# Attention scores of a graph layer: one gather of each pair released a pair earlier, and two products of constants between two groups of products

## The reference

```
xl = (x @ Wl).reshape(-1, HEADS, C)
xr = (x @ Wr).reshape(-1, HEADS, C)
h = jax.nn.leaky_relu(xl[src] + xr[dst], NEG_SLOPE)
e = jnp.einsum('ehc,hc->eh', h, att)
m = jax.ops.segment_max(e, dst, num_segments=N_NODES)
...
msg = alpha[..., None] * xl[src]
out = jax.ops.segment_sum(msg, dst, num_segments=N_NODES)
```

## Time and profile before

| | |
|---|---|
| median of 3 runs | 1267.71 us (1265.4 to 1268.62) |
| the profiled execution | 1267.25 us, its span 1265.2 us |
| score stage, first to last DVE weighting (L1497) | 231.79 to 498.06 us |
| granted TensorE clock over the span | 0.882 |

### The profile page before, as it was taken

How to read it: one execution, slowest core, us unless ns; L and a number is a source line. 1 busy time by engine, 2 the same in 40 slices (tenths; PEclk the granted TensorE clock), 3 DMA queues, 4 the chain that set the end, 5 groups by cost and what they waited for, 6 DMA issues and landing times.

```text
span 1265.2 us, 15650 instructions
## 1 busy us (share of the span) xinstructions
PE 1103.2 (87%) x4847; PEld 815.4 (64%) x4847; DVE 1028.0 (81%) x1458; ACT 678.8 (54%) x1257; POOL 455.9 (36%) x412
## 2 busy tenths in 40 slices
PE   4979878667777775399999999699999999999998
PEld 2578456555556564255555555488888889889896
DVE  8999999778777887899999999876767769573934
ACT  4601200566565663388888888766564674232320
POOL 2072062666665666267777775000002100000000
PEclk9989989676665665599999999799999999999999
DMA  5000000666666667166676776400000111000002
GB/s 189 34 10 15 26 10 7 168 174 175 176 179 169 174 175 183 37 189 194 194 195 195 196 195 142 142 1 26 1 9 26 65 54 31 1 28 15 1 1 83
DMA packets 43434, 122.82 MB, mean 97 GB/s; under 512 B 7838, under 2 KB 8626, under 8 KB 43352
## 3 DMA queue, kind: packets, MB, share of 16 engines
q0 software_dynamic: 29184, 93.81, 28.0%
q1 hardware_dynamic: 14168, 27.98, 6.6%
HBM read 116.13 MB, written 5.59 MB: 96 GB/s over the span
## 4 chain that ended last, share of the span: by engine, by line
PE 46%; ACT 19%; DVE 14%; DMA 7%; issue 7%; POOL 4%; ACTq 1%; SPq 1%; DVEq 0%; POOLq 0%
PE bank L851 11%; PE bank L811 8%; PE bank L797 8%; ACT counts L1037 7%; PE bank L867 7%; DMA arena<-left_table,arena 7%; PE bank L654 5%; POOL arena L570 4%; ACT hot L924 4%; ACT arena L922 4%; PE bank L705 3%; ACT bank L1010 2%; DVE counts L1252 2%; PE bank L759 2%; PE bank L770 1%
## 5 line engine op out<-in xcount | busy, mean ns | idle before, releaser
L570 POOL DMA_INDIRECT arena<-left_table,arena x352 | 375.7, 1067 | 206.2 <-issue 101.6
L759 PE MATMUL bank<-arena,hot 128*128 128x512 f32 x352 | 177.6, 620 | 4.0 <-DVE den_parts L1587 4.0
L705 PE MATMUL bank<-xr_hi,hot_t 128*128 x176 | 114.1, 649 | 73.1 <-ACT bank L1010 50.1
L1497 DVE SCALAR_TENSOR_TENSOR arena<-bank,arena 128x1024 f32<-128x1024 f32 x88 | 107.8, 1225 | 52.3 <-PE bank L705 32.6
L1010 ACT ACTIVATE bank<-arena 128x1024 f32<-128x1024 f32 x88 | 90.4, 1028 | 95.3 <-DMA arena<-left_table,arena 87.3
L851 PE MATMUL bank<-counts_r,ns 128*128 128x512 f32 (+2 forms) x720 | 137.1, 349 | 0.0
L851 PEld LDWEIGHTS bank<-counts_r,ns 128*128 128x128 f32 x720 | 125.6, 188 | 10.4
L1037 ACT ACTIVATE counts<-bank 128x1280 f32 x88 | 108.9, 1238 | 35.0 <-issue 25.8
L770 PE MATMUL bank<-arena 128*128 128x512 bf16 x528 | 113.1, 351 | 0.5 <-ACT counts L1037 0.3
L1499 DVE TENSOR_REDUCE arena<-arena 128x16 f32<-128x1024 f32 x88 | 107.4, 1220 | 3.0
L705 PEld LDWEIGHTS bank<-xr_hi,hot_t 128*128 128x128 f32 x176 | 50.2, 285 | 92.2 <-issue 84.5
(11 more groups left out here) (248 smaller groups left out, 2193.8 us busy)
## 6 DMA issues: line engine op xcount, KB each, us to landing
arena<-left_table,arena POOLq DMA_INDIRECT x352
arena<-in_x_dram SPq DMA_DIRECT2D x18, 256.0 KB, 4.6
arena<-in_L_gnn_W_dram SPq DMA_DIRECT2D x8, 512.0 KB
arena<-in_L_gnn_W_dram SPq DMA_DIRECT2D x2, 1536.0 KB, 10.7
arena<-in_L_gnn_W_dram SPq DMA_DIRECT2D x3, 1024.0 KB, 5.2
left_table<-arena SPq DMA_DIRECT2D x10, 260.0 KB, 2.0
out_dram<-state SPq DMA_DIRECT2D x9, 256.0 KB
arena<-in_L_gnn_Wl_dram SPq DMA_DIRECT2D x1, 1024.0 KB, 9.8
```

Of the source, the lines that this page charges most:

```text
L570: g.indirect_dma_start(out=gathered[n % DEPTH][:, i, :], out_offset=None, in_=left_table, in_offset=bass.IndirectOffsetOnAxis(ap=src_of[:, ...
L705: ins_ = t.matmul(bank[:, 2 * (n % ZRING) + i, :], mine, part[:, bass.ds(at, 1), :].rearrange("p b n -> p (b n)"), start=False, stop=(part ...
L759: t.matmul(bank[:, psum, :], as_float(hot[c % 4]), w[:, i, :], start=(i == 0), stop=(i == 1))
L1497: v.scalar_tensor_tensor(y, bank[:, at:at + 2, :], 0.0, over(att_relu, 1, 2), ALU.max, ALU.mult).then_inc(*rows_weighted.up())
```

## The change

Three edits, all in the score stage.

First, the two gathers of a pair have bounds of their own, LEADS = 4, 3: the first waits for the rows of pair n - 4, the second for those of pair n - 3. In the message stage `gather(n)` is called without bounds, as before. Second, between the four products of a pair's rows and its two linear products stand two products of constants, each 128x128 with 256 columns of the 16-bit ramp, into columns 256 to 511 of bank 7, which nothing reads. Third, the linear terms therefore use only columns 0 to 255 (16 tiles instead of 32): `keep_targets` comes every 8 pairs instead of every 16, 11 times in all instead of 6, and TensorE's wait for it, now ahead of the constants, comes 10 times instead of 5.

```diff
-    LEAD = 3
+    LEADS = 4, 3
...
-    LINEAR_TILES = 512 // (2 * HEADS)
+    LINEAR_TILES = 256 // (2 * HEADS)
...
-            def gather(n):
+            def gather(n, rows=None):
+
                 for i in range(2):
                     c = 2 * n + i
+                    if rows and n + 1 - rows[i] > 0:
+                        g.wait_ge(rows_added.sem, n + 1 - rows[i])
                     g.indirect_dma_start(out=gathered[n % DEPTH][:, i, :], out_offset=None, in_=left_table,
...
                 if n >= DEPTH:
                     g.wait_ge(sources_kept.sem, n - DEPTH + 1)
-                if n >= LEAD:
-                    g.wait_ge(rows_added.sem, n - LEAD + 1)
-                gather(n)
+                gather(n, LEADS)
...
                 ins_.then_inc(*rows_added.up())
+                c = 2 * n
+                if c % LINEAR_TILES == 0 and c:
+                    t.wait_ge(targets_kept.sem, c // LINEAR_TILES)
+
+                for _ in range(2):
+                    t.matmul(bank[:, 7, 256:512], iota_node[:, 0:P], iota_node[:, 0:256], start=True, stop=True)
                 for i in range(2):
                     c = 2 * n + i
                     mine = hot_t[n // 2 % 2][:, (n % 2 * 2 + i) * P:(n % 2 * 2 + i + 1) * P]
-                    if c % LINEAR_TILES == 0 and c:
-                        t.wait_ge(targets_kept.sem, c // LINEAR_TILES)
```

## The result

The changed kernel took 1230.83 us in the median (1228.84 to 1234.4, 4 runs), the kernel before beside it 1268.16 us (1265.4 to 1270.19). The ratio is 0.971 with a 95% interval of 0.9679 to 0.9741: 37 us less, where 30 were forecast, and inside the range. The profiled execution took 1232.27 us, its span is 1230.3.

The account below looks back on a forecast made before the run. A latency, the score stage's round of gather waits, was taken to bound the kernel, not an engine. 87 x (3.06 - 2.715) = 30 us off the profiled 1267.25 gives 1237.2, as a median 1237.5; forecast range 1226 to 1247, widened to 1224 to 1252.

Parts of the forecast that it names:

- The round through the second gather: Score stage: gather, copy, products and release form a loop of waits, three pairs per round, 3.00 us a pair.
- the 1.25 us: Score stage, POOL: the second gather's start behind the first leaves the round, 0.42 us a pair.
- the 0.76 us: Score stage: time from a pair's last product to the start of the gather it releases on POOL, expected to stay.
- 8.99: Score stage: sum in us of the old round's legs, 0.76 + 1.25 + 0.95 + 2.69 + 1.27 + 2.07.
- 2.64: Score stage: us per pair of the round once the second gather is issued first, down from 3.06.
- DVE's floor of 2.51: Score stage: DVE's two operations follow each other at best every 2.51 us, so at most 48 us can be gained.
- a stage that goes back and forth between 2.79 and 2.51: Score stage: TensorE's 2.79 us a pair at low clock alternates with DVE's 2.51 after TensorE catches up at full clock.
- The constants: Score stage, TensorE: two added products cost 0.46 us a pair at low clock, 2.79 in all, and may raise the clock.
- the clock comes back for good: Rival, score stage: TensorE stays at 2.4 GHz, round 6.88 us, DVE's 2.51 binds, 41 to 48 us gained; chance 0.14.
- Landings: Score stage: time for gathers to land after issue taken as unchanged; later than 2.7 to 3 us would show the prediction wrong.
- The half bank: Score stage: five more ACT copies for linear terms, at most 3 us of ACT, costed at nothing.
- 2.715: Score stage: forecast mean us per pair, the middle of the round's 2.64 and TensorE's 2.79.

Follow-up runs that it names:

- the empty slots apart: Changed kernel, but slots without an edge fetch row p of the table (p their partition) instead of row 0: 1221.78 us, ratio 0.9682 to the kernel before.
- the third group: Runs on one chip beside the kernel before (1262.6 us): the changed kernel again, 1228.37 us; with two waits on its second gather, 1232.65; empty slots fetching own rows, 1221.78.

## Why the prediction was right

**The round through the second gather** was the bound, and taking the 1.25 us out of it carried the gain: with the bounds alone the whole gain is there, without them 6 us of it. That mechanism was right.

**The term that was mis-sized is the release.** The prediction kept the 0.76 us as a constant of the round. It is 0.27 for a gather with one wait, and the second gather of the changed kernel has only one. The round is then 8.99 - 1.25 - 0.49 = 7.25, over three 2.42 a pair even at the low clock, below DVE's 2.51; the prediction had 2.64 and so above it. Measured by itself in the kernel before it is worth 11.6 us, in the changed kernel 4.3. The trace before had a hint that the prediction passed over: pair 3, whose gather has no wait for a buffer yet, started 0.27 us after its release.

**DVE's floor of 2.51** was right, and it is where the stage went: 61 steps of 87. The forecast had it only as the lower bound, for stretches at full clock. Its picture, a stage that goes back and forth between 2.79 and 2.51 with TensorE's clock, was not seen: at 0.72 and at 0.89 the same number of steps stood at the floor. Of the 24 steps of the changed kernel that took over 2.6 us, 20 belong to pairs whose copy started 3.9 us or more after issue's end, so to late landings.

**The constants.** Their cost, 0.46 us a pair at the low clock, is what was measured. The 2.79 that TensorE would need was taken as the upper end of the period; it was the wrong thing to average with, because the clock rose further than expected (0.89, not 0.7 to 0.8) and TensorE did not bind. What the clock gave back was likewise of no use: 0.72 and 0.89 gave the same stage. The rival "the clock comes back for good" had the floor that binds, but for another reason: it took 0.86 us out of the round by the clock, and the bounds alone reached the same stage at 0.72. On the clock it was near (0.89).

**Landings.** The prediction took no change. They came 0.2 us later in the median of pairs 3 to 80 (3.06 instead of 2.82 us from issue's end), and at the end of the stage 5 to 6 us, which the prediction had put down to the message stage's gathers behind them. The run with the empty slots apart contradicts that: the same gathers follow there, and the copies of the last five pairs come 2.5 to 4.2 us after issue's end. In the third group the changed kernel's stage stood some 13 us above 87 steps of 2.51; with the empty slots apart some 2 were left. So the landings put at no change are a second mis-sized term. Later than 2.7 to 3 us the prediction had named as a sign of being wrong, and that sign showed.

**The half bank** showed no wait of TensorE for it; it was not run alone.

**The sum.** 30 us were forecast from 87 x (3.06 - 2.715), with 2.715 chosen between two numbers neither of which held. The stage gave 32.8 (2.68 a pair), from a floor at 2.51 for most steps and 15 us above it (233.5 - 87 x 2.51), of which 5.5 in the last five steps. So the direction and the range follow from a mechanism that was right, and that the number came out within 3 us of the stage's gain is luck: a release 0.49 us too long and a cost of the constants that did not bind stood in the sum for the late landings that it left out.

## What to carry to other kernels

Where no engine is full, write down one round of the waits with a duration for each leg, the idle time between a release and the start behind it included, and see which legs the resource that is issued last brings in; releasing two things that leave together by bounds of their own takes the first one's issue out of the round. Count the waits on the instruction at the release, and leave out one that another covers. Products of constants to raise TensorE's clock paid here only while TensorE's products lay in the binding round; test the two apart. Let padded slots of a gather fetch different rows.

## What the runs showed of the hardware that was not expected

A gather on GpSimd that waits for two semaphores started 0.76 us after the product that released it, most often and never sooner, one that waits for one most often 0.27 us, whichever gather of a pair it was. Ahead of the one with two waits the trace has a semaphore instruction of its own.

At the stage's end, where the gathers of empty slots fetch one and the same row of the table, the DMA engines were busy at a share of 1.00 for 155 GB/s; with different rows in those slots at 0.73 for 206 GB/s.

How long TensorE had stood idle did not tell by itself at which level its clock came back. In the changed kernel the first product of a pair took 0.79 us, the lower level's time, after idle times of 2.19, 2.23 and 2.43 us (274.2, 301.0, 448.8), but 0.49 us, the higher level's, after 2.15 and 2.42 us (395.9, 248.1); in the kernel before it took 0.49 or 0.50 after 2.12 to 2.54 us (four places).
